# One gathered tile row in every third block moved from GpSimd's gathers to 128 single-row loads on SyncE, the overflow flag made earlier, block 1 prepared at earlier steps

## What is computed

```python
transformed = jnp.einsum('ni,rio->rno', h, weight)   # weight 16 x 256 x 256
msg = transformed[rel_type, src] * norm
out = jax.ops.segment_sum(msg, dst, num_segments=h.shape[0])
x = _layernorm(x + out, axis=-1)
```

## Time and profile before

| | |
|---|---|
| median of 3 runs | 2064.54 us (2063.78 to 2065.51) |
| profiled execution | 2063.79 us, span 2062.1 us |
| PE busy | 1956.9 us, 95% |
| POOL busy | 1536.0 us, 74% |
| DVE busy | 1272.3 us, 62% |
| ACT busy | 273.4 us, 13% |
| gathers by POOL (L533) | 1614 and 4, 947 ns each |
| mean clock granted to PE | 0.992 |

### The profile page before, as it was taken

One profiled execution on the slowest core, in us unless ns is written; L12 is line 12 of the kernel. 1 busy time (PEld: TensorE's weight loads), 2 busy tenths in 40 slices (PEclk: granted clock), 3 DMA queues, 4 the chain that ended last, 5 costly groups with the idle time before them and its releaser, 6 DMA issues.

```text
span 2062.1 us, 33712 instructions
## 1 busy us (share of the span) xinstructions
PE 1956.9 (95%) x11962; PEld 1817.7 (88%) x11962; DVE 1272.3 (62%) x3579; ACT 273.4 (13%) x557; POOL 1536.0 (74%) x1649
## 2 busy tenths in 40 slices
PE   6899999999999999999999999999999999999997
PEld 5799999898889889988888899888998999898886
DVE  5767666566656665666565666666666666666653
ACT  1211111111111111111111111111111111111110
POOL 7777777777777777777777777777777777777773
PEclk8999999999999999999999999999999999999999
DMA  6434433343434343334333433343333433433332
GB/s 210 138 112 117 115 113 117 113 114 114 117 112 113 114 118 113 113 113 118 113 113 113 118 113 114 113 118 113 114 112 115 116 113 112 117 115 114 110 111 64
DMA packets 107716, 239.01 MB, mean 116 GB/s; under 512 B 31226, under 2 KB 55642, under 8 KB 107482
## 3 DMA queue, kind: packets, MB, share of 16 engines
q0 software_dynamic: 77760, 212.43, 35.9%
q1 hardware_dynamic: 29342, 21.02, 3.5%
q10 hardware_dynamic: 440, 3.32, 0.4%
HBM read 230.23 MB, written 9.72 MB: 116 GB/s over the span
## 4 chain that ended last, share of the span: by engine, by line
PE 43%; POOL 31%; issue 14%; DMA 7%; DVE 2%; POOLq 2%; SPq 0%; ACT 0%
POOL rows L533 31%; PE ps_a L952 29%; PE ps_z L915 9%; DMA rows<-in_x,idx 7%; PE ps_z L917 4%; POOLq L575 1%; DVE spread L752 1%; DMA w_raw<-in_L_gnn_weight 0%; PE ps_m L899 0%; DVE a_lo L728 0%; SPq L455 0%; ACT a_hi L830 0%; DVE w_parts L741 0%; POOLq L576 0%; SPq L456 0%
## 5 line engine op out<-in xcount | busy, mean ns | idle before, releaser
L533 POOL DMA_INDIRECT rows<-in_x,idx x1614 | 1527.8, 947 | 494.9 <-issue 473.2
L952 PE MATMUL ps_a<-spread,rows 128*128 128x96 f32 (+7 forms) x8604 | 1602.1, 320 | 82.6 <-DMA rows<-in_x,idx 53.6
L952 PEld LDWEIGHTS ps_a<-spread,rows 128*128 128x128 f32 x8604 | 1311.8, 192 | 203.0 <-DVE spread L752 87.8
L752 DVE TENSOR_SCALAR spread<-ps_i,key,meta 128x96 f32<-128x96 f32 (+8 forms) x2141 | 812.8, 447 | 62.0 <-PE ps_a L952 62.0
L915 PE MATMUL ps_z<-w_parts,a_hi 128*128 128x512 f32 x1568 | 810.2, 518 | 1.0 <-DVE a_lo L728 1.0
L728 DVE TENSOR_TENSOR a_lo<-ps_a,a_hi 128x512 fp32r<-128x512 f32 x392 | 251.8, 684 | 636.8 <-ACT a_hi L830 636.8
L917 PE MATMUL ps_z<-w_parts,a_lo 128*128 128x256 f32 x1568 | 439.7, 280 | 0.0
L830 ACT ACTIVATE a_hi<-ps_a 128x512 fp32r<-128x512 f32 x392 | 212.3, 594 | 1176.0 <-PE ps_a L952 1176.0
L915 PEld LDWEIGHTS ps_z<-w_parts,a_hi 128*128 128x128 f32 x1568 | 299.4, 191 | 5.0 <-DVE a_lo L728 1.1
L917 PEld LDWEIGHTS ps_z<-w_parts,a_lo 128*128 128x128 f32 x1568 | 299.8, 191 | 1.8
L808 ACT ACTIVATE meta<-ps_m 128x160 f32<-128x160 f32 (+1 forms) x49 | 14.8, 303 | 349.7 <-PE ps_m L899 349.7
(11 more groups left out here) (69 smaller groups left out, 152.8 us busy)
## 6 DMA issues: line engine op xcount, KB each, us to landing
rows<-in_x,idx POOLq DMA_INDIRECT x1614, 2.8
xr<-in_x SPq DMA_DIRECT2D x48, 128.0 KB
out<-z_rows SPq DMA_DIRECT2D x48, 128.0 KB
w_raw<-in_L_gnn_weight SPq DMA_DIRECT2D x16, 256.0 KB, 3.3
raw<-packed SPq DMA_DIRECT2D x192, 20.0 KB
packed<-in_src ACTq DMA_DIRECT2D x1, 805.7 KB, 5.7
packed<-in_dst ACTq DMA_DIRECT2D x1, 805.7 KB, 7.2
packed<-in_edge_type ACTq DMA_DIRECT2D x1, 805.7 KB, 9.1
```

What stands on the lines that cost most here:

```text
L533: pool.indirect_dma_start(rows[:, row, :], None, x, bass.IndirectOffsetOnAxis(ap=index, axis=0)).then_inc(arrived, 16)
L752: dve.tensor_scalar(spread[:, n % RING, 0:width], iota[:, 0:width], key[:, b % SLOTS, step.column:step.column + 1], meta[:, b % SLOTS, 3, ...
L952: ins = pe.matmul(ps_a[:, g % OPEN, h, (begin - zero) * R:(stop - zero) * R], rows[:, step.row, h * P:(h + 1) * P], spread[:, n % RING, (b ...
```

## The change

Three edits. First, in blocks 4, 7, ... 46 (`HELPED`) tile row 36 (`HELPED_ROW`, the seventh of the last part) isn't gathered by POOL. SP loads the tile's 128 source indices into `near_src` (`open_tile`) and issues 128 loads of one row of x each into `near_rows`, with addresses from registers that are loaded eight at a time. These loads are spread over three blocks, in five stages of 8, 40, 16, 40 and 24 rows (`FETCH`), before and after SP's wait for `rows_normalised`; the last stage is issued in the helped block itself. PE waits for `near_rows_in` and reads `near_rows` at that step. Second, the flag is made at steps 12 to 18 of block 47, and SP loads it before it waits for its last store. Third, in block 0 the four steps that prepare block 1 come at steps 14 to 17 in the place of 18 to 23, the seek steps after the edge count one or two steps sooner, and the weights at steps 12 to 33 in the place of 13 to 33.

The diff (without the declarations of the semaphores `near_src_in` and `near_rows_in`):

```diff
--- before.py
+++ after.py
@@ -150,22 +150,27 @@
     ends_before = [sum(1 for end in ends if end < n) for n in range(len(flat))]
     EVAC_LAG = 4
+    HELPED = [b for b in range(4, NB - 1) if b % 3 == 1]
+    HELPED_ROW = BT - PT + 6
+    AT_ONCE = 8
+    FETCH = (8, 40, 16, 40, 24)
     SLOTS = 3
     CONVERT, TURN, COPY, KEYS = range(4)
-    FIRST_PREPARE = (18, 20, 21, 23)
+    FIRST_PREPARE = (14, 15, 16, 17)
     SECOND_PREPARE = (1, 2, 4, 6)
     PREPARE = (18, 21, 26, 31)
     AHEAD = 2
-    SEEK_ROW, SEEK_GATHER, SEEK_EDGE, SEEK_TURN, SEEK_TABLE, SEEK_COUNTS, SEEK_COPY = 2, 8, 10, 11, 12, 13, 14
-    WEIGHTS_AT = {13 + n * 22 // R: n for n in range(R)}
+    SEEK_ROW, SEEK_GATHER, SEEK_EDGE, SEEK_TURN, SEEK_TABLE, SEEK_COUNTS, SEEK_COPY = 2, 8, 10, 9, 11, 12, 13
+    WEIGHTS_AT = {12 + n * 23 // R: n for n in range(R)}
     WEIGHTS_BEFORE = 2
     SURE = 8
     CONFIRM = 3
     PRODUCT_FROM = 6
     NORM_AT = 10
+    ENDED_AT, TOTAL_STEP, FLAG_AT = 12, 14, 18
     def products_at(b, t):
         if b == NB - 1:
@@ -299,6 +304,8 @@
         hit_dst = spare[:, 0:2 * SROW].bitcast(I32).rearrange("p (q e) -> p q e", q=2)
         bound_row, first_tile, first_near = (spare[:, n:n + BOUNDS]
                                              for n in range(2 * SROW, 2 * SROW + 3 * BOUNDS, BOUNDS))
+        near_rows = below[:, 0:2, :].rearrange("p c b -> p (c b)")[:, 0:F]
+        near_src = below[0:1, 2, 0:P].bitcast(I32)
         hit_cmp = z_rows.rearrange("p n f -> p (n f)")[:, 0:2 * SROW].rearrange("p (q e) -> p q e", q=2)
         ps_f = ps_m[:, 256:512]
@@ -418,7 +427,11 @@
         def own_tiles(b):
-            return [step.row for step in plan[b] if step.column < BT]
+            return [step.row for step in plan[b] if step.column < BT and not helped(b, step.row)]
+
+        def helped(b, row):
+
+            return b in HELPED and row == HELPED_ROW
         def pair(row):
             return row // PT * (SURE // 2) + row % PT // 2
@@ -456,6 +469,31 @@
                     sp.dma_start(raw[PT * s:PT * s + PT, :, :],
                                  packed[:, bass.ds(first, PART_EDGES)].rearrange("a (j p) -> j a p", p=P)).then_inc(
                                      edges_in, 16)
+
+            def open_tile(b):
+
+                if b > HELPED[0]:
+                    sp.wait_ge(tiles_summed, signals(row_done[b - 3, HELPED_ROW]))
+                n = GROUPS * b - 1
+                first = sp.value_load(first_i[0:1, n:n + 1], min_val=0, max_val=E)
+                sp.dma_start(near_src[:, :], packed[0:1, bass.ds(first + HELPED_ROW % PT * P, P)]).then_inc(
+                    near_src_in, 16)
+                sp.wait_ge(near_src_in, 16 * (HELPED.index(b) + 1))
+
+            def fetch_rows(b, chunk):
+
+                tile = next((h for h in HELPED if h - 3 <= b < h), None)
+                stage = {(-3, 1): 0, (-2, 0): 1, (-2, 1): 2, (-1, 0): 3, (-1, 1): 4}.get((b - tile, chunk)) if tile else None
+                if stage is None:
+                    return
+                if stage == 0:
+                    open_tile(tile)
+                for p in range(sum(FETCH[:stage]), sum(FETCH[:stage + 1]), AT_ONCE):
+                    _, found = nc.values_load_multi_w_load_instructions(
+                        near_src[0:1, p:p + AT_ONCE], engines=[mybir.EngineType.SP], min_val=0, max_val=N - 1)
+                    for q, row in enumerate(found):
+                        sp.dma_start(near_rows[p + q:p + q + 1, :], x[bass.ds(row, 1), :]).then_inc(
+                            near_rows_in[HELPED.index(tile) % 2], 16)
             def raw_left(b):
@@ -494,17 +532,21 @@
                 if b + 3 < NB:
                     raw_left(b + 3)
                     load_edges(b + 3)
+                fetch_rows(b, 0)
                 sp.wait_ge(rows_normalised, b)
                 rows_of = min(SB, N - b * SB)
                 sp.dma_start(out[(b - 1) * SB:b * SB, :], z_out[:, :]).then_inc(rows_out, 16)
                 sp.dma_start(xr[0:rows_of, :], x[b * SB:b * SB + rows_of, :]).then_inc(own_rows_in, 16)
+                fetch_rows(b, 1)
             sp.wait_ge(rows_normalised, NB)
             EVEN = LAST // 16 * 16
             sp.dma_start(out[(NB - 1) * SB:N - LAST + EVEN, :], z_out[0:EVEN, :]).then_inc(rows_out, 16)
             sp.dma_start(out[N - LAST + EVEN:N, :], z_out[EVEN:LAST, :]).then_inc(rows_out, 16)
+            flag = uncounted(sp)
             sp.wait_ge(rows_out, (NB + 1) * 16)
+            return flag
         def fast_pool(pool):
             pool.memset(ident[:, :], 0.0).then_inc(constants_made, 1)
@@ -733,6 +775,16 @@
             def tile_block(b, sums, products, rows_):
                 for t in range(length[b]):
                     n = start_of[b] + t
+                    if b == NB - 2 and t == ENDED_AT:
+
+                        dve.wait_ge(blocks_counted, NB)
+                        dve.sem_inc(count_ended, 1)
+                    if b == NB - 2 and t == FLAG_AT:
+                        dve.wait_ge(flag_steps, 1)
+                        dve.tensor_scalar(flag_f[:, :], ps_f[0:1, TOTAL_AT:TOTAL_AT + 1], float(E), None,
+                                          ALU.not_equal).then_inc(flag_steps, 1)
+                        dve.wait_ge(flag_steps, 2)
+                        dve.tensor_copy(flag_i[:, :], flag_f[:, :]).then_inc(flag_steps, 1)
                     if sums:
                         if b == 0 and t in WEIGHTS_AT:
                             w = WEIGHTS_AT[t]
@@ -776,13 +828,6 @@
             seek = {SEEK_ROW: seek_row, SEEK_EDGE: seek_edge, SEEK_TABLE: seek_table, SEEK_COPY: seek_copy}
             blocks(dve, tile_block)
-            dve.wait_ge(blocks_counted, NB)
-            dve.sem_inc(count_ended, 1)
-            dve.wait_ge(flag_steps, 1)
-            dve.tensor_scalar(flag_f[:, :], ps_f[0:1, TOTAL_AT:TOTAL_AT + 1], float(E), None,
-                              ALU.not_equal).then_inc(flag_steps, 1)
-            dve.wait_ge(flag_steps, 2)
-            dve.tensor_copy(flag_i[:, :], flag_f[:, :]).then_inc(flag_steps, 1)
         def runs(values):
@@ -924,6 +969,10 @@
                 for t in range(length[b]):
                     if sums:
                         n, step = start_of[b] + t, plan[b][t]
+                        if b == NB - 2 and t == TOTAL_STEP:
+                            pe.wait_ge(count_ended, 1)
+                            pe.matmul(ps_f[0:1, TOTAL_AT:TOTAL_AT + 1], total[:, :], ones[:, :], start=True,
+                                      stop=True).then_inc(flag_steps, 1)
                         for ahead in prepared(b, t, TURN):
                             turn_edges(ahead)
                         if b == 0 and t == SEEK_TURN:
@@ -934,7 +983,10 @@
                         pe.wait_ge(spreads_made, n + 1)
                         if step.row not in arrived:
                             arrived.add(step.row)
-                            if b == 0 or step.row % PT < SURE:
+                            if helped(b, step.row):
+                                h = HELPED.index(b)
+                                pe.wait_ge(near_rows_in[h % 2], 16 * P * (h // 2 + 1))
+                            elif b == 0 or step.row % PT < SURE:
                                 if arrival(b, step.row) not in arrived:
                                     arrived.add(arrival(b, step.row))
                                     pe.wait_ge(*arrival(b, step.row))
@@ -951,7 +1003,7 @@
                                     zero -= SB
                                 ins = pe.matmul(
                                     ps_a[:, g % OPEN, h, (begin - zero) * R:(stop - zero) * R],
-                                    rows[:, step.row, h * P:(h + 1) * P],
+                                    (near_rows if helped(b, step.row) else rows[:, step.row, :])[:, h * P:(h + 1) * P],
                                     spread[:, n % RING, (begin - step.first) * R:(stop - step.first) * R],
                                     start=opens[part] == n, stop=False, skip_group_check=True)
                         if n in ends:
@@ -966,10 +1018,6 @@
             turn_edges(0)
             seek_count()
             blocks(pe, tile_block)
-
-            pe.wait_ge(count_ended, 1)
-            pe.matmul(ps_f[0:1, TOTAL_AT:TOTAL_AT + 1], total[:, :], ones[:, :], start=True, stop=True).then_inc(
-                flag_steps, 1)
         def uncounted(eng):
@@ -1137,8 +1185,8 @@
         @block.sync
         def _(sp):
-            fast_sync(sp)
-            with sp.If(uncounted(sp) == 1):
+            flag = fast_sync(sp)
+            with sp.If(flag == 1):
                 general_sync(sp)
         @block.gpsimd
```

More of the change, by code:

```diff
@@ L383, in build @@
         late_in = [sem(f"late_in{s}") for s in range(GROUPS)]
+        near_src_in = sem("near_src_in")
+        near_rows_in = [sem(f"near_rows_in{n}") for n in range(2)]
         weights_in = [sem(f"weights_in{n}") for n in range(2)]
```

## The result

The changed kernel is slower: 2183.53 us median (4 runs, 2178.53 to 2187.62) against 2065.03 us; the ratio is 1.0573, 95% interval 1.0555 to 1.0592. That is outside the predicted range of 2031 to 2090 and on its other side. The profiled execution took 2187.62 us with a span of 2185.9 us. In seven of the eleven sets of runs behind this document the kernel before itself took 2500 to 2550 us instead of 2065, for a reason that stays open, and nothing is concluded from the ratios of those sets.

What follows compares the result with a forecast made beforehand. POOL's gathers were taken to set the pace from about 330 us on. 2063.79 less 18.75 (gathers), 3.2 (block 1 sooner) and 7.3 (flag) gave 2034.5; plus 0.75 and 1 for jitter, 2036 us, range 2031 to 2090.

Steps and rivals of the forecast that it cites:

- The bound and the value of a gather: POOL's gathers set the pace from about 330 us on; each removed saves 1.25 us, fifteen save 18.75 us.
- the smaller edits: Block 1 prepared sooner saves 3.2 us on POOL; the flag made in block 47 saves 7.3 us at the end.
- Checked once ... I take 0.62: the rows tie a check to a load.: SP's batched register load is checked once for eight rows, so a row costs SP 0.62 us.
- the price named for that, 0.85: SP's row loads: with the batch checked per value, a row costs 0.85 us.
- rival A: At PE's wait for near_rows_in at row 36: SP can't keep up, 2292 us at 0.85 a row; chance 0.20.
- The limit of 0.71: SP's last stage in the helped block: SP meets PE's deadline up to 0.71 us a row.
- The loop of 38 + 120c: SP, PE's stop at row 36, next normalisation, SP's next start: 38 + 120c us for three blocks sets the pace.
- the formula 2035 + 15 x (loop - 122.9): End time if SP is late: 15 times the loop's excess over POOL's 122.9 us for three blocks, added to 2035.
- The rule on register loads: SP's batched load at about 200 ns a register: a row would cost 0.76 us, the end near 2130 us.
- The rule on the DRAIN: DRAINs at the program's ends take some 12 ns, so the early flag wins nothing; set aside for POOL's 8.65 us row.

Runs made afterwards that it cites:

- e5: The changed kernel with the bounds checks of its batched register loads left out; 2035.76 us against 2066.06 for the kernel before, ratio 0.9857.
- e10: The changed kernel, still fetching all rows with checks, but POOL gathers row 36 too and PE reads that copy; 2053.97 us against 2064.55, ratio 0.9950.
- e12: The changed kernel with bounds checks left out in every second batch of eight; 2036.15 us against 2066.25 for the kernel before, ratio 0.9854.
- e14: The changed kernel with bounds checks kept in three of four batches; 2098.30 us against 2065.89 for the kernel before, ratio 1.0163.

## Why the prediction was wrong

- **The bound and the value of a gather: right.** e5 has POOL's pace of the earlier trace rows less the fifteen gathers: 2035.8 us against the 2036 forecast with c (SP's time for a row) below the limit. From e10 to e5 the gathers give 18.2 us where 18.75 was forecast; the smaller edits give 10.6 together where it was 10.5.
- **The step that failed: "Checked once ... I take 0.62: the rows tie a check to a load."** In the earlier trace rows each load has one value, so eight loads beside eight checks can't tell "per load" from "per value". The batch is checked per value, 1553 checks to 195 loads, and a row took 0.775 to 0.785 us. Of the price named for that, 0.85, the DMA was over-sized (0.226 and not 0.330 for one row) and the load under-sized (0.776 for eight registers and not 0.480). With one check a batch, 0.62 would have been too much as well: e5 has 0.52 with none.
- **The mechanism: right, as rival A.** The limit of 0.71 lies between e12 (0.785 - 56/120 x 0.255 = 0.67 a row) and e14 (0.73). The loop of 38 + 120c gives 131.0 at 0.775 and 132.2 at 0.785; 131.9 was measured. That the 38 fits (131.9 - 94.2 = 37.7) is in part luck, for its terms are off both ways: SP starts its raw loads 12.2 us after the store and not 14 (the earlier trace rows already show 13.4), and the last row lands 1.2 us after its issue and not 2.8; but a later raw load takes 5.4 us and not 4.5, and PE needs 12.9 us from row 36 to the next store and not 10.6.
- **The size of A: too small.** At 0.775 the formula 2035 + 15 x (loop - 122.9) gives 2157; 2183.5 was measured. With the measured loops it gives 2170, and 2087 for e14, which took 2098. What is left, 13 and 11 us, comes for the most part from the pace that it sets the loop against, POOL's 122.9 in every block. But up to some 390 us PE runs at 38.7 us a block in e5, since POOL is still ahead, and the loop takes that too. From block 2's normalisation to block 45's, 43 blocks, POOL's pace would be 1761 us; e5 takes 1750.5, 11 less, e14 1812.0 and the changed kernel 1901.7. The differences to e5, 61.5 and 151.2, are near those of the medians, 62.5 and 147.8.
- **The chances.** 0.20 for A was too little: the code passes the bounds with the batched load just as with the single one, and the trace showed such a check beside every value ever loaded.
- **The rule on register loads.** The Trainium skill, "Runtime: NRT & Kernel Launch", section "Instruction fetch mechanics", has about 200 ns a register. Here eight registers took 0.776 us where one took 0.480: 42 ns for each further one. The measurement decides; the rule doesn't hold for this load. That its 0.76 us a row and 2130 us came nearer than 0.62 and 2036 is chance: it had no check for each value and too dear a load.
- **The rule on the DRAIN.** The Trainium skill, "VectorE: DVE Perf Modes", section "The DRAIN you can't avoid", has some 12 ns; POOL's takes 8.65 us in the earlier trace rows. The trace disagrees, and 7.6 us were there to be won.

The version that beats both kernels is e5's, 1.4% faster than before. It is safe only where the inputs hold no node number outside the table, and so is e12's, which takes the same time and still checks half of the numbers.

## What to carry to other kernels

Work moved to an idle queue has two limits: the sum that fits in its free time, and the deadline of the piece that is issued last. Work out the loop through the engine that waits for it, and see on which side of the threshold the uncertain unit price puts it; here 0.07 us a row (e12 against e14) was all that lay between 30 us won and 32 lost. Where a trace shows an operation only one at a time, its side instructions may belong to the operation or to the value: count what the new form would issue for both before choosing one, and choose the dearer where the loss beyond the threshold is the steeper.

## What the runs showed of the hardware

POOL's DRAIN ends 8.5 to 8.7 us after POOL's last gather or after it is reached, whichever is later. Before it was reached at 2053.2, long after the gathers, and ended at 2061.9. In the changed kernel it is reached during the gathers; from the end of the last gather (timeline of POOL) to the DRAIN's end at 2131.2 + 14.8 = 2146.0 are 8.5 us, and in e5, e10, e12 and e14 it is 8.5 to 8.7 as well:
```profile
2136.52 0.95 POOL L575 DMA_INDIRECT rows<-in_x,idx  x1 [0.30 <-issue]
```
After PE's wait of 13 us the granted clock stands at its lower level. Windows of the changed kernel (length, busy us of each engine, clock, DMA share, GB/s), the first before the wait, the others behind it:
```profile
1016.00:1020.00 4.00, 4.00 (x27) 3.88 (x26) 3.42 (x8) 0.94 (x2) 3.02 (x4) 1.00 0.47 139
1033.00:1038.00 5.00, 3.11 (x9) 2.79 (x10) 0.00 (x0) 0.00 (x0) 0.00 (x0) 0.50 0.07 22
1038.00:1042.00 4.00, 4.00 (x25) 3.86 (x24) 0.00 (x0) 0.51 (x2) 0.28 (x1) 0.75 0.06 12
1042.00:1046.00 4.00, 4.00 (x25) 3.92 (x24) 3.85 (x9) 0.57 (x2) 3.09 (x4) 1.00 0.26 72
```
0.50 is 1.2 GHz, 1.00 is 2.4. The four matmuls of row 36 behind the wait took 1.94 us, the same four in e5, without a wait, 0.97. From there to the next store are 12.9 us in the changed kernel and 10.3 in e5 (1076.37 to 1086.65), so each missed deadline costs some 2.6 us more than the wait itself. The blocks say the same: 54.5 - 38.7 - 13.2 = 2.6.
